# TensorE's loop over pairs of experts in a mixture-of-experts kernel, written out as a straight program

## The chip, the cores and the metric

The kernel runs on one core of one Trainium2 chip. Times are device microseconds of that core, and lower is better. The kernel before takes 859.89 us, the median of three runs (859.68 to 860.04 us).

## The reference, cut to what matters

Tokens (4 batches of 1024, 512 wide) pass a linear layer whose weights and bias are chosen by the batch's category. Each row then goes to one of 8 experts by the largest of 8 softmax probabilities. An expert takes at most 512 tokens, the first that chose it; a token beyond that gets nothing. The result is scaled by the probability and added to the input.

```python
h = einsum('bsd,bdh->bsh', x, W[cat]) + b[cat][:, None, :]
xf = h.reshape(4096, 512)
probs = softmax(xf @ Wr); eidx = argmax(probs); p_tok = probs[eidx]
rank = position of the token among those that chose the same expert
keep = rank < 512                       # capacity 4096 / 8
xe = xf[dispatch]                       # (8, 512, 512)
hid = maximum(einsum('ecd,edf->ecf', xe, W1), 0.0)   # F = 2048
ye = einsum('ecf,efd->ecd', hid, W2) * p
out = x + scatter_add(ye)
```

## The kernel before, in words

Every engine has a program of its own, written out by hand, and the engines meet at semaphores; no scheduler moves anything. All large products are made of float32 values split in two parts, a high part and the rest, and each product is three matmuls (high by high, high by low, low by high: `PARTS`).

The first stage, up to the 153rd microsecond, is a straight program on all engines: the linear layer for 32 tiles of 128 tokens, the routing, and the table of which token goes to which slot. The `pe.wait_ge` calls there compare with constants.

The second stage is the experts, two (`par` 0 and 1) in each of the four iterations of a loop (`pair`), L913. For one expert TensorE makes 16 hidden tiles of 128 x 512 (`j`, L931 to L945): 4 blocks of the contraction times 3 parts is 12 matmuls a tile, into two PSUM banks in turn (`acc_ps`). Between them `second(q)` (L915 to L929) makes 48 matmuls that add a quarter of the hidden rows into the output banks `y_ps`. The order is tiles 0 to 7, second(0), tiles 8 to 11, second(1), tiles 12 to 15, second(2), second(3): 192 matmuls at L941 and 192 at L924 for each expert, so 768 in one iteration.

TensorE waits in this loop for: the split weights (`s_w1lo`, L935, and `s_w2lo`, L916), a freed hidden bank (`s_accf`, L936, which asks that the tile before the last has been taken out), the split inputs of the expert (`s_xelo`, L939), and at the expert's first `second` the outputs of the last expert read (`s_y`, L918). Since `pair` is a register there, each of these thresholds is computed by TensorE's sequencer: register instructions stand among the matmuls.

The other engines go as before in loops of their own: ScalarE takes out a hidden tile (L511) and makes high parts of weights (L459, L465); VectorE makes the low part of the hidden tile and frees its bank (L717), the low parts of weights (L624, L630), and at an expert's end scales the four output tiles and adds the residual (L740). Both loop over pairs, four iterations. SyncE loads the weights in a loop over experts. GpSimd gathers and scatters rows, in a straight program.

Of the kernel before, what the change touches and what calls it, by code (L numbers as in the profile page):

```python
# [17 lines left out]
def moe_kernel(nc, x, x_t, cat, cond_w, cond_wt, cond_b, cond_br, w_r, w_1, w_2, out, h_rows):  # L18
# [8 lines left out]
    E = w_r.shape[1]  # L27
# [41 lines left out]
    with ctx:  # L69
# [674 lines left out]
        def _(pe):  # L744
# [165 lines left out]
                if s < SB - 1:  # L910
                    keep_warm(KEEP_BLOCK)

            with pe.Fori(0, E // 2) as pair:  # L913
                for par in range(2):
                    def second(q):  # L915
                        pe.wait_ge(s_w2lo, pair * (4 * QN) + 2 * (par * QN + q + 1))  # L916
                        if q == 0:
                            pe.wait_ge(s_y, pair * (2 * SB) + par * SB + 1)  # L918
                        pe.wait_ge(s_accf, NT + pair * (2 * FT) + par * FT + QF * (q + 1))
                        for s in range(SB):  # L920
                            for jj in range(QF):
                                j = q * QF + jj
                                for a, w in PARTS:
                                    last = nc.tensor.matmul(y_ps[:, s, :], hts[:, j % HB, a, s * P:(s + 1) * P],  # L924
                                                            w2s[:, q % 2, w, jj, :],
                                                            start=(j == 0 and (a, w) == (HI, HI)),
                                                            stop=(j == FT - 1 and (a, w) == (LO, HI)))
                            if q == QN - 1:
                                last.then_inc(s_f2, 1)  # L929

                    for j in range(FT):  # L931
                        slot, jj = (j // QF) % 2, j % QF
                        tile = pair * (2 * FT) + par * FT + j
                        if jj == 0:
                            pe.wait_ge(s_w1lo, pair * (4 * QN) + 2 * (par * QN + j // QF + 1))  # L935
                        pe.wait_ge(s_accf, NT - 1 + tile)  # L936
                        for k in range(DK):
                            if j == 0:
                                pe.wait_ge(s_xelo, pair * (2 * DK) + par * DK + k + 1)  # L939
                            for w, a in PARTS:  # L940
                                last = nc.tensor.matmul(acc_ps[:, j % 2, :], w1s[slot][:, w, k, jj * P:(jj + 1) * P],  # L941
                                                        xts[:, par, a, k, :],
                                                        start=(k == 0 and (w, a) == (HI, HI)),
                                                        stop=(k == DK - 1 and (w, a) == (LO, HI)))
                        last.then_inc(s_acc, 1)  # L945
                        if jj == QF - 1 and j // QF >= 1:
                            second(j // QF - 1)
                    second(QN - 1)
# [34 lines left out]
```

## Time and profile before

| | before |
|---|---|
| median of three runs | 859.89 us |
| the profiled execution, its own time | 859.88 us |
| its span, first to last instruction | 858.1 us |
| mean granted TensorE clock | 0.993 of 2.4 GHz |
| TensorE matmul busy | 832.0 us (97%) |
| VectorE, ScalarE, GpSimd busy | 47%, 30%, 27% |

The profile is of one execution. Matmuls overlap in the records: one of 512 columns is shown as 389 ns long, while a block of 48 takes 10.88 us from the end of the block before to its own end, so one goes in each 0.227 us. "issue" as a releaser means that the engine stood idle and the profile shows nothing that it waited for. The code that an engine's sequencer runs comes by DMA too, in queues of the kind "instruction".

### The profile page before, as it was taken

How to read it: one execution, taken by the hardware profiler on the slowest of the kernel's cores; microseconds unless marked ns; L12 is line 12 of the kernel's file. 1: busy time of each engine (PE TensorE's matmuls, PEld its weight loads, DVE VectorE, ACT ScalarE, POOL GpSimd, SP SyncE). 2: the span in 40 equal slices, each digit the busy share in tenths (PEclk: the TensorE clock that was granted, in tenths of full speed). 3: DMA queues.
4: the chain of work that ended last, by engine and by line, in shares of the span. 5: the costliest groups of instructions: out<-in, count | busy, mean ns of one | idle time of the engine just before them, and what ended most of it. 6: DMA issues, size and time to landing. Idle time of an engine off the chain costs nothing.

```text
span 858.1 us, 10370 instructions
## 1 busy us (share of the span) xinstructions
PE 832.0 (97%) x3909; PEld 673.2 (78%) x3909; DVE 403.5 (47%) x557; ACT 255.3 (30%) x345; POOL 229.7 (27%) x238
## 2 busy tenths in 40 slices
PE   8959998999999999999999999999999999999997
PEld 5636786788888887888888878888888788888886
DVE  5645663644354434453455336533653275327431
ACT  4412210533143313332233224322432143205320
POOL 2000002724530453036302630173017301021201
PEclk9979999999999999999999999999999999999999
DMA  9847344373435333733263335432544253234201
GB/s 321 293 158 269 137 149 146 138 256 125 133 119 212 123 123 100 245 116 129 91 244 115 132 98 198 151 130 88 196 152 133 95 172 143 86 122 160 102 1 50
DMA packets 60820, 127.68 MB, mean 149 GB/s; under 512 B 8235, under 2 KB 8235, under 8 KB 60258
## 3 DMA queue, kind: packets, MB, share of 16 engines
q1 hardware_dynamic: 46706, 93.35, 30.2%
q0 software_dynamic: 13488, 32.54, 11.8%
q10 hardware_dynamic: 576, 1.05, 0.4%
q8 instruction: 40, 0.66, 0.3%
q14 instruction: 10, 0.08, 0.0%
HBM read 110.13 MB, written 25.17 MB: 158 GB/s over the span
## 4 chain that ended last, share of the span: by engine, by line
PE 94%; DMA 3%; DVE 1%; issue 1%; POOL 0%; ACT 0%; SPq 0%; POOLq 0%
PE acc_ps L941 41%; PE y_ps L924 41%; PE acc_ps L856 6%; PE tp_ps L856 3%; DMA stage<-cond_w 2%; PE tp_ps L783 1%; PE y_ps L792 1%; PE acc_ps L840 1%; DVE select L617 0%; PE tp_ps L758 0%; DMA rows<-h_rows,tok_all 0%; PE y_ps L816 0%; POOL rows L367 0%; PE tp_ps L840 0%; PE y_ps L840 0%
## 5 line engine op out<-in xcount | busy, mean ns | idle before, releaser
L941 PE MATMUL acc_ps<-xt_split,w_split 128*128 128x512 f32 x1536 | 352.9, 389 | 4.6 <-issue 3.5
L924 PE MATMUL y_ps<-w_split,xt_split 128*128 128x512 f32 x1536 | 352.1, 389 | 0.0
L941 PEld LDWEIGHTS acc_ps<-xt_split,w_split 128*128 128x128 f32 x1536 | 288.1, 188 | 65.4 <-issue 4.4
L924 PEld LDWEIGHTS y_ps<-w_split,xt_split 128*128 128x128 f32 x1536 | 288.3, 188 | 59.9
L511 ACT ACTIVATE xt_split<-acc_ps 128x512 fp32r<-128x512 f32 x128 | 76.5, 598 | 420.4 <-PE acc_ps L941 420.4
L717 DVE SCALAR_TENSOR_TENSOR xt_split<-acc_ps,xt_split 128x512 fp32r<-128x512 f32 x128 | 88.6, 692 | 210.8 <-ACT xt_split L511 210.8
L374 POOL DMA_INDIRECT rows<-h_rows,idx_all x112 | 117.1, 1045 | 254.5 <-DVE tp_ps L707 218.2
L624 DVE TENSOR_TENSOR w_split<-stage,w_split 128x1024 fp32r<-128x1024 f32 x66 | 80.9, 1226 | 16.4 <-ACT w_split L459 16.4
L740 DVE SCALAR_TENSOR_TENSOR rows<-y_ps,p_cur,rows 128x512 f32<-128x512 f32 x32 | 24.0, 751 | 133.0 <-PE y_ps L924 133.0
L630 DVE TENSOR_TENSOR w_split<-stage,w_split 128x1024 fp32r<-128x1024 f32 x64 | 78.5, 1226 | 16.4 <-ACT w_split L465 16.4
L406 POOL DMA_INDIRECT out<-rows,put_all x32 | 31.5, 983 | 154.3 <-DVE rows L740 154.3
L459 ACT ACTIVATE w_split<-stage 128x1024 fp32r<-128x1024 f32 x66 | 69.4, 1053 | 0.0
L465 ACT ACTIVATE w_split<-stage 128x1024 fp32r<-128x1024 f32 x64 | 67.4, 1053 | 0.0
L856 PE MATMUL acc_ps<-w_split,xt_split 128*128 128x512 f32 x228 | 57.3, 402 | 0.0
L856 PEld LDWEIGHTS acc_ps<-w_split,xt_split 128*128 128x128 f32 x228 | 42.4, 191 | 13.5 <-issue 3.3
L399 POOL DMA_INDIRECT out<-b_rows,drop_all x32 | 32.8, 1026 | 56.9 <-DMA b_rows<-x 47.8
L367 POOL DMA_INDIRECT rows<-x,tok_all x32 | 34.7, 1085 | 26.3 <-DMA out<-rows,put_all 15.8
L362 POOL DMA_DIRECT2D h_rows<-rows x7 | 5.5, 790 | 119.6 <-DVE rows L566 119.6
L707 DVE STREAM_TRANSPOSE tp_ps<-rows 128x512 f32<-128x512 f32 x32 | 32.8, 1070 | 0.0
L498 ACT ACTIVATE xt_split<-tp_ps 128x512 fp32r<-128x512 f32 x32 | 19.1, 597 | 42.6 <-DVE tp_ps L707 42.6
L566 DVE TENSOR_TENSOR rows<-acc_ps,b_rows 128x512 f32<-128x512 f32 x21 | 14.4, 690 | 26.4 <-PE acc_ps L856 22.7
L856 PE MATMUL tp_ps<-w_split,xt_split 128*128 128x512 f32 x108 | 26.7, 396 | 0.0
(113 smaller groups left out, 260.6 us busy)
## 6 DMA issues: line engine op xcount, KB each, us to landing
stage<-w SPq DMA_DIRECT2D x64, 1024.0 KB, 5.6
b_rows<-x SPq DMA_DIRECT2D x8, 1024.0 KB, 7.7
h_rows<-rows POOLq DMA_DIRECT2D x7, 1024.0 KB, 4.7
stage<-cond_wt SPq DMA_DIRECT2D x4, 1024.0 KB, 7.8
x_more<-x_t SPq DMA_DIRECT2D x4, 1024.0 KB, 7.9
stage<-x_t SPq DMA_DIRECT2D x3, 1024.0 KB, 6.1
stage<-cond_w SPq DMA_DIRECT2D x3, 1024.0 KB, 9.3
rows<-h_rows,idx_all POOLq DMA_INDIRECT x112, 2.7
```

Source lines behind the costliest of these rows:

```text
L367: pool.indirect_dma_start(out=rows[:, which, s, :], out_offset=None, in_=source, in_offset=bass.IndirectOffsetOnAxis(ap=tok_all[:, e, s:s ...
L374: pool.indirect_dma_start(out=h_quart[:, t * P:(t + 1) * P], out_offset=None, in_=h_parts, in_offset=bass.IndirectOffsetOnAxis(ap=idx_all[ ...
L399: pool.indirect_dma_start(out=out, out_offset=bass.IndirectOffsetOnAxis(ap=drop_all[:, BATCH * e + t:BATCH * e + t + 1], axis=0), in_=b_ro ...
L459: nc.scalar.activation(w1s[slot][:, HI, ks, :], stage[:, slot, ks, :], ACTF.Copy).then_inc(s_w1hi, 1)
L465: nc.scalar.activation(w2s[:, slot, HI, ks, :], stage[:, 2 + slot, ks, :], ACTF.Copy).then_inc(s_w2hi, 1)
L511: nc.scalar.activation(hts[:, j % HB, HI, :], acc_ps[:, j % 2, :], ACTF.Relu).then_inc(s_hhi, 1)
L624: nc.vector.tensor_tensor(w1s[slot][:, LO, ks, :], stage[:, slot, ks, :], w1s[slot][:, HI, ks, :].bitcast(f32), ALU.subtract).then_inc(s_w ...
L630: nc.vector.tensor_tensor(w2s[:, slot, LO, ks, :], stage[:, 2 + slot, ks, :], w2s[:, slot, HI, ks, :].bitcast(f32), ALU.subtract).then_inc ...
L717: nc.vector.scalar_tensor_tensor(hts[:, j % HB, LO, :], acc_ps[:, j % 2, :], 0.0, hts[:, j % HB, HI, :].bitcast(f32), ALU.max, ALU.subtrac ...
L856: last = nc.tensor.matmul(cond_bank(n), xts[:, c % 4, a, k, t * P:(t + 1) * P], w2s[:, (c // CPB) % 2, w, k, :], start=(k == 0 and (a, w) ...
L924: last = nc.tensor.matmul(y_ps[:, s, :], hts[:, j % HB, a, s * P:(s + 1) * P], w2s[:, q % 2, w, jj, :], start=(j == 0 and (a, w) == (HI, HI)),
L941: last = nc.tensor.matmul(acc_ps[:, j % 2, :], w1s[slot][:, w, k, jj * P:(jj + 1) * P], xts[:, par, a, k, :], start=(k == 0 and (w, a) == ...
```

## The change

One line. The loop over `pair` on TensorE is no longer a loop of the machine but one of Python, so the builder writes the body four times, one after the other, with `pair` a number.

```diff
-            with pe.Fori(0, E // 2) as pair:
+            for pair in range(E // 2):
                 for par in range(2):
                     def second(q):
                         pe.wait_ge(s_w2lo, pair * (4 * QN) + 2 * (par * QN + q + 1))
```

The 3072 matmuls of the expert stage are the same and in the same order. The branches go, with all register instructions, and waits compare with constants. The instructions of the other four engines stay as they are.

On TensorE, this is the end of the loop's body before, and behind it the body's start, to which the branch goes back (`y_ps` are the output banks, `acc_ps` the hidden ones):

```order
L924 MATMUL y_ps<-w_split,xt_split 128x512 [waits acc_free]
L924 MATMUL y_ps<-w_split,xt_split 128x512 x47
L913 REGISTER_ALU
L913 COMPARE_AND_BRANCH
```

```order
L913 ISA
L936 ISA [waits w1_lo_done]
L939 ISA [waits acc_free]
L941 MATMUL acc_ps<-xt_split,w_split 128x512 [waits xe_lo_done]
L941 MATMUL acc_ps<-xt_split,w_split 128x512 x2
L939 REGISTER_ALU
L941 MATMUL acc_ps<-xt_split,w_split 128x512 [waits xe_lo_done]
```

The first ends in the branch; the second begins with three fused register instructions. At the same place of the changed program, where the second pair of experts begins:

```order
L924 MATMUL y_ps<-w_split,xt_split 128x512 [waits acc_free,w2_lo_done]
L924 MATMUL y_ps<-w_split,xt_split 128x512 x47
L941 MATMUL acc_ps<-xt_split,w_split 128x512 [waits xe_lo_done,acc_free,w1_lo_done]
L941 MATMUL acc_ps<-xt_split,w_split 128x512 x2
L941 MATMUL acc_ps<-xt_split,w_split 128x512 [waits xe_lo_done]
```

The matmuls follow each other with no branch and no register instruction; the same semaphores are waited for. A second place is hidden tile 4 of each expert, on TensorE, where the weights change from one slot to the other. Before:

```order
L935 REGISTER_ALU
L936 REGISTER_ALU [waits w1_lo_done]
L941 MATMUL acc_ps<-xt_split,w_split 128x512 [waits acc_free]
L941 MATMUL acc_ps<-xt_split,w_split 128x512 x11
```

And now:

```order
L941 MATMUL acc_ps<-xt_split,w_split 128x512 [waits acc_free,w1_lo_done]
L941 MATMUL acc_ps<-xt_split,w_split 128x512 x11
```

Before, a register instruction carried the wait for the weights and the matmul the one for the hidden bank (`acc_free`). Now a wait instruction of its own stands ahead of the matmul with `acc_free`, and the matmul carries the wait for the weights. In the first stage nothing moved.

## Rows read from the trace of the kernel before

**Rows 1.** Page, busy time of each engine, share of the span, instructions
```profile
PE 832.0 (97%) x3909; PEld 673.2 (78%) x3909; DVE 403.5 (47%) x557; ACT 255.3 (30%) x345; POOL 229.7 (27%) x238
```
**Rows 2.** Page, costliest groups: busy us, mean ns, idle before, releaser
```profile
L941 PE MATMUL acc_ps<-xt_split,w_split 128*128 128x512 f32 x1536 | 352.9, 389 | 4.6 <-issue 3.5
L924 PE MATMUL y_ps<-w_split,xt_split 128*128 128x512 f32 x1536 | 352.1, 389 | 0.0
```
**Rows 3.** Chain that ended last, whole span: start us, us, what
```profile
152.59 22.09 PE acc_ps L941 x96
174.67 10.88 PE y_ps L924 x48
...
305.23 21.76 PE y_ps L924 x96
326.99 1.73 PE acc_ps L941 x7
328.73 1.31 issue
330.04 20.36 PE acc_ps L941 x89
...
504.31 1.15 issue
...
679.74 1.07 issue
```
**Rows 4.** TensorE's timeline around the three steps back, and between two experts
```profile
239.79 6.51 PE L941 MATMUL acc_ps<-xt_split,w_split 128*128 128x512 f32 x28
...
326.83 1.90 PE L941 MATMUL acc_ps<-xt_split,w_split 128*128 128x512 f32 x7
...
502.56 1.75 PE L941 MATMUL acc_ps<-xt_split,w_split 128*128 128x512 f32 x7
...
677.99 1.75 PE L941 MATMUL acc_ps<-xt_split,w_split 128*128 128x512 f32 x7
```
**Rows 5.** VectorE's timeline: between two experts, three steps back, and the end
```profile
243.34 0.69 DVE L717 SCALAR_TENSOR_TENSOR xt_split<-acc_ps,xt_split 128x512 fp32r<-128x512 f32 x1 [2.60 <-ACT xt_split L511]
...
327.03 0.75 DVE L740 SCALAR_TENSOR_TENSOR rows<-y_ps,p_cur,rows 128x512 f32<-128x512 f32 x1 [1.97 <-PE y_ps L924]
332.03 0.69 DVE L717 SCALAR_TENSOR_TENSOR xt_split<-acc_ps,xt_split 128x512 fp32r<-128x512 f32 x1 [4.25 <-ACT xt_split L511]
...
507.45 0.69 DVE L717 SCALAR_TENSOR_TENSOR xt_split<-acc_ps,xt_split 128x512 fp32r<-128x512 f32 x1 [3.94 <-ACT xt_split L511]
...
682.79 0.69 DVE L717 SCALAR_TENSOR_TENSOR xt_split<-acc_ps,xt_split 128x512 fp32r<-128x512 f32 x1 [3.85 <-ACT xt_split L511]
...
853.52 0.75 DVE L740 SCALAR_TENSOR_TENSOR rows<-y_ps,p_cur,rows 128x512 f32<-128x512 f32 x1 [1.97 <-PE y_ps L924]
```
**Rows 6.** DMA queues, whole run: packets, MB, share of 16 engines
```profile
q8 instruction: 40, 0.66, 0.3%
```
**Rows 7.** The same queue from 332 to 498 us
```profile
q8 instruction: 6, 0.10, 0.2%
```
**Rows 8.** The same queue from 499 to 501 us
```profile
q8 instruction: 1, 0.02, 2.9%
```
**Rows 9.** The same queue from 502 to 504 us
```profile
q8 instruction: 1, 0.02, 4.4%
```
**Rows 10.** The same queue from 506 to 508 us
```profile
q8 instruction: 1, 0.02, 3.0%
```
**Rows 11.** TensorE's waits from 152 to 855 us: total us, times, longest
```profile
PE acc_ps L941 <- issue: 3.5, 3, 1.3
PE acc_ps L941 <- DVE xt_split L693: 1.1, 1, 1.1
```
**Rows 12.** The instruction queue from 0 to 152 us, the first stage
```profile
q8 instruction: 6, 0.10, 0.3%
```
**Rows 13.** Chain from 150 to 175 us: the hand-over into the expert stage
```profile
151.84 0.70 DVE xt_split L693
152.54 0.04 issue
```

## The prediction, made before the changed kernel ran

> **What bounds the kernel now.** I read the engines' busy shares first. TensorE is busy 97% of the span and the next engine, VectorE, 47% [rows 1]: the time is TensorE's own, and only its idle time or fewer, faster matmuls can change it. Then the costliest groups. The two lines of the expert stage, 1536 matmuls each, are most of it; L924 has no idle time before it at all, and L941 has 4.6 us, of which 3.5 us is "issue", time in which TensorE waited for nothing that the profile shows [rows 2]. TensorE's waits from 152 us on say the same in another way: three issue gaps, and one wait of 1.1 us for VectorE when the stage begins [rows 11]. Nothing else ever holds TensorE there: no weight load, no bank, no gather.
>
> The chain tells where the three gaps are. It is TensorE alone, in blocks of 48 matmuls that take 10.88 us each, or 21.76 us for 96. After 305.23 us come the last 96 of the first pair; the second pair begins at 326.99, runs 7 matmuls, and stands still for 1.31 us. The same happens at 504.31 (1.15 us) and at 679.74 (1.07 us) [rows 3]. The reader should see that they come once per step back of the loop, always after 7 matmuls, and nowhere else.
>
> What is TensorE waiting for? The code itself. The queue of kind "instruction" brings 40 packets in the whole run, 0.66 MB, so 16 KB each [rows 6]. Inside a pair they come evenly: 6 in the 166 us from 332 to 498 [rows 7], one in about 28 us, and the stretches of the same length in the other pairs hold 6 too. At the step back there are three close together: one in 499 to 501, one in 502 to 504, one in 506 to 508 [rows 8 to 10], and TensorE, which stopped at 504.31 until 505.46 [rows 3], lies between the second and the third. I read this as: the sequencer, some microseconds ahead of the array, takes the branch and has the piece of code with the body's start fetched (first packet); that piece ends a few instructions after the body's start; the next must be fetched (second packet), and the 7 matmuls at hand run out before it can be used. In the straight stretches the next piece is there before it is needed, and a new piece costs nothing that can be seen: between 174.67 and 326.99 the blocks are 10.88 or 21.76 us long without exception.
>
> **The change, part by part.** First, the branches. Three steps back go. What each costs in all (the gap and small slips beside it) I take from three whole iterations. The last reading of output tiles by VectorE, released by the last matmul of a pair, starts at 327.03 us for the first pair and at 853.52 us for the fourth [rows 5]: 526.49 us for three pairs. Three times 768 matmuls are 48 blocks of 48, at 10.88 us [rows 3], 522.24 us. The excess is 4.25 us, 1.42 us a step back. The gaps alone sum to 1.31 + 1.15 + 1.07 = 3.53 us; the rest is that a matmul's record reaches 0.16 us beyond the start of the next (0.389 less 0.227) three times, and slips such as the one at the first step, where the 7 matmuls take 1.90 us and at the other two 1.75 us [rows 4]. I take 4.25 us, since the time between the two releases holds all of it; 3.53 is its lower bound.
>
> Does something stay behind? In the first iteration, which has no step back, TensorE starts at 152.59 [rows 3] and the second pair at 326.83 [rows 4], 174.24 us for 174.08 us of blocks: 0.16 us, the waits for the first inputs. That remains. If it were the cost of any pair's beginning, the three others would keep it, and the gain would be 3.77 us. For the others the inputs are there long before, so I don't take it.
>
> The fetching of code stays, spread evenly: the stage from 152.59 to 853.5 is then 697 us long, at one packet in 28 us some 25 packets, and with the 6 of the first stage [rows 12] some 31 in place of 40. Each is hidden by the piece that is running. If one were not hidden, it would cost something like the 1.42 us that it costs after a branch.
>
> Second, the register instructions. They stand ahead of the matmuls at each tile, and L924 and L941 show no gap at them [rows 2, 11]: the array has work queued while the sequencer computes. I count them at nothing gained. The wait instructions that take their place at some tiles are counted at nothing too. L924 has such waits already in the loop and no idle time [rows 2]. The one that differs is hidden tile 4: the sequencer now stands at `acc_free`. Between two experts VectorE frees tile 0's bank at 243.34 + 0.69 = 244.03 [rows 5]; tile 2, which needs it, starts two tiles of 2.72 us after 239.79 [rows 4], at 245.23. So 1.20 us of cover at each tile, and a hand-over from VectorE to an idle TensorE took 0.04 us [rows 13]. It would cost only if that hand-over took more than 1.20 us; I bound it by 0 and by 8 tiles times 0.04.
>
> Third, the other engines. ScalarE and VectorE keep their own steps back, and these now lose the cover that TensorE's gap gave them. What must be ready: tile 0 of the new pair must be taken out before tile 2 starts, 5.44 us after the pair's first matmul. In the trace VectorE ended it at 332.72, 508.14 and 683.48 [rows 5], which is 5.89, 5.58 and 5.49 us after 326.83, 502.56 and 677.99 [rows 4]. So even if VectorE could not have been a moment earlier, TensorE would wait only 0.45 + 0.14 + 0.05 us, and three hand-overs, 0.76 us in all. But VectorE was held there by ScalarE, and ScalarE by TensorE itself: VectorE had been idle for 4.25 us [rows 5], and without the gap would have been called 1.3 us earlier. I take 0 and keep 0.76 for the range. Weight loads, gathers and scatters are set off by work that runs behind TensorE, so they move with it; none of them made TensorE wait once [rows 11], and per pair of 175 us they get 1.4 us less.
>
> The end is unchanged: from VectorE's last reading at 853.52 to the end of the span, 4.6 us.
>
> Sum: 859.88 us (the profiled execution; the median of the runs is 859.89, the same) less 4.25 is 855.63 us. Bounds: with 4.5 us gained, 855.4; with 3.53 us gained and all 0.76 + 0.32 us of new waits, 857.4.
>
> The page "Runtime: NRT & Kernel Launch" of the Trainium skill, in "Instruction fetch mechanics", says that a taken branch whose target is not in the window at hand makes the sequencer fetch it first, and that prefetch is purely sequential; by this rule the gaps go with the branches, and the trace agrees with three packets round each one. The same section gives TensorE an instruction memory of 128 KiB, 2048 instructions. The loop's body has fewer (1536 for its 768 matmuls and weight loads, and some tens of others), so if it stayed in that memory a step back would fetch nothing; the trace disagrees, since the 6 packets come in every pair. By the first rule the sum stands at 855.6 us; by the second the gap would not be a fetch, and rival (a) would hold.
>
> **The rivals.** (a) The gap is not the code's fetch but some other cost of beginning a pair, and stays: the change then doesn't do what it says. What speaks for it: "issue" names no cause. Against: the beginning of the first pair lacks it, 174.24 us against 175.73 for the second (502.56 less 326.83), and so does the middle of a pair, where the same waits stand. Only what the branch itself takes would go. In the trace that could be the slip of 0.15 us (1.90 less 1.75) at the first step [rows 4]; three of them make 0.45 us, and the time 859.4 us. A reading of the page "Advanced Engine Details and Errata", "Control Flow Timing", leads the same way: it has a compare-and-branch at about 108 ns, by which three would give back about 0.3 us; no row here shows such a duration by itself. Chance 6%.
>
> (b) The straight program can't be fetched in time: slower. Place: each of the about 25 new pieces of code of the stage. Price: if each stops TensorE as the one after a branch does, 25 x 1.42 = 35.5 us, less 4.25, and the time is 891 us. It decides from 0.17 us a piece on. For it: the fetch after a branch takes longer than 7 matmuls. Against: TensorE ran through 24 such pieces inside the four iterations and 6 in the straight first stage [rows 12], and no gap recurs with them. Chance 3%.
>
> (c) A wait takes the gap's place: VectorE's or ScalarE's own step back, uncovered. At most 0.76 us by the working above, so the time is 856.4 us, still faster. Chance 9%.
>
> **How the numbers follow.** The forecast, 855.6 us, has 82%, with (c) 9%, (a) 6% and (b) 3%. From the run spread of 0.2 us either way, a little more for the same first stage in another build, and the bounds above, the range is 855.0 to 857.0. A difference of less than 0.2%, 1.7 us, can't be told from no change here; the forecast and (c) lie beyond it, (a) within, (b) on the other side. So faster 0.91, same 0.06, slower 0.03.
>
> **What would show it right or wrong.** In the changed profile: no issue gap at L941 at all, or none over 0.2 us; the pairs 174.1 us apart; the span 853.9 us; about 31 packets in the instruction queue, evenly spaced; VectorE's idle time before the first L717 of a pair back near 2.6 us. Wrong: a gap of about 1 us after a few matmuls of a pair, or a wait for L717 at the third tile of a pair (c), or short gaps every 28 us (b).

## The result, and the profile after

The changed kernel takes 857.01 us (median of 8 executions, 854.65 to 858.47), the kernel before beside it 859.96 us (8 executions). The ratio is 0.9962, 95% interval 0.9947 to 0.9977: faster, by 2.95 us between the medians. Forecast were 855.6 us and a range of 855.0 to 857.0; the median lies a hundredth beyond its upper end. By the ratio the gain is 3.3 us, where 4.25 were forecast. Two later comparisons on other chips gave 0.9948 (0.9934 to 0.9963) and 0.9947 (0.9931 to 0.9964), which is 4.5 us; between the medians it is 4.0 and 4.8 us. All ratios and intervals leave out three executions of a slower state (893.68 us with 16 added instructions, 4214.43 us with 224, 2163.0 us of the kernel before); the medians given do not.

The costliest groups of the changed kernel's page, busy us, mean ns, idle before and its releaser. They answer to [rows 2]:

```profile
L941 PE MATMUL acc_ps<-xt_split,w_split 128*128 128x512 f32 x1536 | 352.2, 389 | 1.1 <-DVE xt_split L693 1.1
L924 PE MATMUL y_ps<-w_split,xt_split 128*128 128x512 f32 x1536 | 352.1, 389 | 0.0
```

The matmuls cost what they did. The 3.5 us of "issue" before L941 is gone, and what is left is the wait for the first inputs of the stage, which was there before [rows 11]. The chain (start, us, what) answers to [rows 3]:

```profile
154.34 22.05 PE acc_ps L941 x96
...
328.71 21.76 PE acc_ps L941 x96
...
502.79 21.76 PE acc_ps L941 x96
...
676.87 21.76 PE acc_ps L941 x96
```

The reader is to see blocks of 96 at a pair's beginning, whole, where there were 7 matmuls, a gap and 89. Pairs follow each other at 174.08 us (502.79 less 328.71, 676.87 less 502.79). VectorE's timeline shows the first hidden tile of the second pair and the last reading of outputs, as in [rows 5]:

```profile
332.10 0.69 DVE L717 SCALAR_TENSOR_TENSOR xt_split<-acc_ps,xt_split 128x512 fp32r<-128x512 f32 x1 [2.60 <-ACT xt_split L511]
...
850.98 0.75 DVE L740 SCALAR_TENSOR_TENSOR rows<-y_ps,p_cur,rows 128x512 f32<-128x512 f32 x1 [1.97 <-PE y_ps L924]
```

VectorE's idle time there fell from 4.25 to 2.60 us, what it is in the middle of a pair. And the instruction queue over the whole run, which answers to [rows 6]:

```profile
q8 instruction: 31, 0.51, 0.2%
```

From the first matmul of the expert stage to VectorE's last reading it was 853.52 less 152.59, 700.93 us; now it is 850.98 less 154.34, 696.64 us. So the stage gave back 4.29 us where 4.25 were forecast. But it starts 1.75 us later (154.34, not 152.59), and so the span fell only from 858.1 to 855.6 us. The loss lies in a first stage whose instructions are the same. Below, "the expert stage" is always this interval.

### The profile page after: what moved, and what is told of

Its sections match the earlier page's. It is cut to its first block, busy times and chain, and to the rows that moved or that the text cites. A ratio compares the mean times of both kernels' runs of the same rounds, so it can differ in the third digit from the quotient of the medians.

```text
span 855.6 us, 10205 instructions
## 1 busy us (share of the span) xinstructions
PE 832.2 (97%) x3909; PEld 674.9 (79%) x3909; DVE 403.5 (47%) x557; ACT 255.2 (30%) x345; POOL 229.7 (27%) x238
## 3 DMA queue, kind: packets, MB, share of 16 engines
q10 hardware_dynamic: 576, 1.05, 0.4%
## 4 chain that ended last, share of the span: by engine, by line
PE 95%; DMA 3%; DVE 1%; issue 0%; ACT 0%; SPq 0%; POOL 0%; POOLq 0%
PE acc_ps L941 41%; PE y_ps L924 41%; PE acc_ps L856 6%; PE tp_ps L856 3%; DMA stage<-cond_w 2%; PE tp_ps L783 1%; PE y_ps L792 1%; PE acc_ps L840 1%; DVE select L617 0%; PE tp_ps L758 0%; DMA rows<-h_rows,tok_all 0%; PE y_ps L816 0%; PE y_ps L888 0%; PE acc_ps L865 0%; PE tp_ps L840 0%
## 5 line engine op out<-in xcount | busy, mean ns | idle before, releaser
L941 PE MATMUL acc_ps<-xt_split,w_split 128*128 128x512 f32 x1536 | 352.2, 389 | 1.1 <-DVE xt_split L693 1.1
L941 PEld LDWEIGHTS acc_ps<-xt_split,w_split 128*128 128x128 f32 x1536 | 288.3, 188 | 61.1 <-issue 1.3
L717 DVE SCALAR_TENSOR_TENSOR xt_split<-acc_ps,xt_split 128x512 fp32r<-128x512 f32 x128 | 88.5, 692 | 206.9 <-ACT xt_split L511 206.9
```

The lines of the kernel that those rows point to most:

```text
L717: nc.vector.scalar_tensor_tensor(hts[:, j % HB, LO, :], acc_ps[:, j % 2, :], 0.0, hts[:, j % HB, HI, :].bitcast(f32), ALU.max, ALU.subtrac ...
```

## The experiments

The text on record speaks of "pieces of code": what one packet of the instruction queue brings. The straight program has 7,919 TensorE instructions in its trace and takes 31 packets of 16 KB, about 256 instructions each. The loop's body has 1,593 (768 matmuls with a weight load each, and 57 others), which is 6.2 pieces. Of these, 19 stand ahead of the point where TensorE stops in the kernel before: three register instructions, seven matmuls with their weight loads, and two more register instructions. So the first piece ends some 20 instructions behind the body's start, and the body lies in 1 + 7 = 8 pieces. The places given below all follow from this 20. Three things could make the gap: the step back itself, the fetch of the branch's target, or the fetch of the piece behind it. They differ in what happens if the loop is kept and the code is only shifted. All kernels here compute the reference in full.

**The kernel before, unchanged.**

> The kernel before, unchanged, to see how its own time spreads. Theory (the step back costs 1.42 us, and the first stage varies by itself from one execution to the next): the time from the first matmul of the expert stage to the last is 701 us again, three gaps of 1.1 to 1.3 us after 7 matmuls, median 859.9 us; whatever differs between executions lies before the expert stage (loads of the first weights, the clock in the two long waits). Rival (the loop's version has a steadier first stage than the straight one): all executions within 0.3 us of 859.9.

Measured: 867.25 us beside 866.64 for the same kernel, ratio 1.0014 (0.9999 to 1.0029). This chip is slower than the first, so neither the 859.9 us nor the 701 us of the theory was met. On it both versions of the kernel also wait some 0.7 us at L941 six times, which the profiles on the other chips don't show; the profile puts five of the six here, and two in the changed kernel, to the freeing of a bank (L717), and the others to nothing that it shows. The gaps are there, 1.60, 1.20 and 1.28 us after 7 matmuls, and 40 packets; the expert stage takes 707.70 us. The executions run from 865.85 to 872.73 us, so the rival of a steadier loop version is out.

**24 instructions that do nothing, ahead of the loop.**

```diff
+            for _ in range(48):
+                pe.wait_ge(s_mask, 13)
             with pe.Fori(0, E // 2) as pair:
```

Two such waits make one instruction. They were satisfied long before.

> The kernel before, loop kept, with 24 more instructions that do nothing (waits already satisfied) on TensorE just ahead of the loop, so that the body's start stands 24 places later in the code. Theory (the gap is the fetch of the SECOND 16 KB piece of code after the branch, which comes too late since the first ends some 20 instructions behind the body's start): the body now starts at the head of a piece, the piece after it is needed only 28 us later, and the three gaps go although every branch stays: expert stage 696.6 us plus at most three slips of 0.25 us, median about 856, as the straight program. Rival A (the gap is the cost of the branch or of the pair's beginning): three gaps of 1.1 to 1.3 us stay, 859.9 us. Rival B (it is the fetch of the branch's target): the gaps stay or move to the very first matmul, 859.9 us.

Measured: 864.96 us, ratio 0.9983 (0.9962 to 1.0004); expert stage 702.61 us, 5.1 us shorter than in the kernel before on this chip. No gap at any step back, with every branch in place. By time alone this run can't be told from no change, since the interval reaches 1.0004. But the instruction queue says something that the theory hadn't:

```profile
q8 instruction: 13, 0.21, 0.1%
```

Thirteen packets for the whole run, and none after 321 us: from the second pair on the body is not fetched again at all. Shifted by 24, it starts 4 instructions behind the head of a piece and lies in 7 pieces; before, it lay in 8. So this run can't tell a late second piece from code that stayed. The wait before the first L941 was 2.37 us, in place of 1.05, so the 24 instructions cost some 1.3 us where they stood. That is part of why the total gained less than the stage.

**16 such instructions.** The same edit with 32 waits.

> As with 24, but 16 such instructions, so that the piece ends 4 instructions behind the body's start. Theory: TensorE has no matmul at hand in place of 7 while the second piece comes, so each step back costs 7 x 0.227 = 1.59 us more, 3.0 in place of 1.42: the gap stands at the first matmul of the pair, expert stage 705.6 us, median 859.9 + 4.8 = 864.7 us. Rival A and B: 859.9 us.

Measured: 882.01 us (878.03 to 893.68), ratio 1.0184 (1.0140 to 1.0227), some 16 us by the ratio and 12 us between the profiled executions (878.16 and 865.92 us), where the theory gave 4.8. TensorE's timeline where the second, third and fourth pair begin:

```profile
335.97 24.68 PE L944 MATMUL acc_ps<-xt_split,w_split 128*128 128x512 f32 x96 [3.27 <-issue]
...
517.48 21.95 PE L944 MATMUL acc_ps<-xt_split,w_split 128*128 128x512 f32 x96 [2.48 <-issue]
...
695.95 23.55 PE L944 MATMUL acc_ps<-xt_split,w_split 128*128 128x512 f32 x96 [2.23 <-issue]
```

The gap stands at the first matmul and is longer, as the theory has it, with 40 packets. What it had missed is behind the gap: the 96 matmuls take up to 24.68 us in place of 21.95. The windows around 336 us (stretch, TensorE busy, matmuls, granted clock, DMA share, GB/s) tell why:

```profile
336.00:339.00 3.00, 3.00 (x8) 0.50 0.19 69
339.00:342.00 3.00, 3.00 (x9) 0.53 0.60 158
342.00:345.00 3.00, 3.00 (x15) 1.00 0.66 191
```

After 3.27 us of idle time TensorE's clock stood at its lower level, 1.2 GHz, for some 6 us: a longer gap can cost the clock too. It is not by length alone: behind the gap of 2.48 us the granted clock stayed at 1.00, behind the one of 2.23 us it was 0.63 and 0.80 in the next two stretches of 3 us. The expert stage took 717.82 us, 10.1 more than on the same chip before: 8.0 us of gaps against 4.1, some 4.3 us of slow clock behind two of them, and 1.5 us of two waits in the first pair. In this profile the stage also starts 2.1 us later. That late start isn't explained, nor is why others of its executions took as long as 889.43 us.

**The changed kernel again.**

> The changed kernel, unchanged again, on the same chip as the kernel before. Theory: the expert stage takes 696.6 us again without any gap, and the scatter of the earlier runs (854.7 to 858.5) lies in the first stage, the same scatter that the kernel before has: median of enough runs 855.7 us, ratio 0.995. Rival (the straight program makes the first stage about 1.3 us longer, where a step of clock or a load falls otherwise): the first matmul of the expert stage starts about 1 to 2 us later than in the kernel before in this profile too, and the ratio stays at 0.9965.

Measured: 862.62 us, ratio 0.9948 (0.9934 to 0.9963). Expert stage 702.30 us, against 707.70: 5.40 us less, of which 4.08 are the three gaps of that profile. This profile starts it at 155.36 us, 3.5 us later than the kernel before, so a late start came a second time, while the ratio was already the forecast one.

**224 such instructions, spread over two idle times of the first stage.** This is the run that separates the late second piece from code that stays.

```diff
             keep_warm(KEEP_FIRST)
+            for _ in range(200):
+                pe.wait_ge(s_mask, 2)
...
             def route(c):
+                if c == CPB:
+                    for _ in range(248):
+                        pe.wait_ge(s_mask, 13)
```

> The loop kept, and 224 instructions that do nothing on TensorE, spread over its two idle times in the first stage (before the first tiles and before the ninth-microsecond wait at the second batch), so that the loop's body starts 52 places ahead of the end of a 16 KB piece of code (256 instructions) in place of 20, and still lies in 8 pieces, as in the kernel before. Theory 1 (the fetch of the second piece comes too late, and a body in 8 pieces doesn't stay in the memory): 40 or 41 packets again, all fetched anew at each step back, but some 20 matmuls (4.5 us) at hand while the second comes: no gap, expert stage as in the straight program. Theory 2 (what took the gaps away with 24 was only that a body in 7 pieces isn't fetched again): the gaps stay wherever the body is fetched again, 1.4 us each. If only 13 or 14 packets come, the limit isn't 8 pieces.

Measured: 41 packets, so the body was fetched anew for each pair. The instruction queue, and TensorE's waits from 160.5 to 862 us:

```profile
q8 instruction: 41, 0.67, 0.3%
PE acc_ps L946 <- DVE xt_split L693: 1.0, 1, 1.0
```

No gap. The expert stage took 696.99 us, that of the straight program within 0.4. The time, 864.43 us (ratio 1.0036, 1.0023 to 1.0050), is the price of 224 instructions in the first stage: the expert stage starts at 161.18 us. They were not free in the idle times, as I had thought they would be. Theory 1 stands: the gap is the second piece coming too late, and a step back with a fetch costs nothing if some 20 matmuls stand before the piece's end.

The start times of the packets in the traces give the margin. In all thirteen gaps (three each in the two profiles of the kernel before and in those with 8 and with 16 instructions, one in the loop with one step back) TensorE goes on 2.3 to 3.0 us after the second piece's packet has started (at the second step back of the kernel before, packet 502.61, matmul 505.46). Here that packet starts at 335.53 us, as the pair's first matmul does, so by the same times the piece can be used at 338.6 at the latest, while the matmuls at hand last until about 340.5 (an estimate: 22 of them at 0.227 us).

**One step back in place of three.**

```diff
-            with pe.Fori(0, E // 2) as pair:
-                for par in range(2):
+            with pe.Fori(0, E // 4) as quad:
+                for half in range(2):
+                    pair = quad * 2 + half
+                    for par in range(2):
```

> The loop with two iterations of two pairs each, so one step back in place of three; the body starts at the same place of the code. Theory: one gap of 1.1 to 1.6 us after 7 matmuls of the third pair, none at the second and fourth; the expert stage 2.8 us shorter than in the kernel before; some 34 packets. Rival (a pair's beginning costs the gap): three gaps.

Measured: 858.41 us, ratio 0.9974 (0.9961 to 0.9986), 34 packets, and one gap, at the third pair. Its waits from 300 us on:

```profile
PE acc_ps L943 <- issue: 1.4, 1, 1.4
```

Expert stage 698.25 us: 2.7 less than before, 1.65 more than straight. One step back costs one gap; the rival, a gap at each pair's beginning, is out.

**The 24 instructions at a place where TensorE is idle** (behind the first `keep_warm`, where the last run had 100 of its 224).

> The loop kept, and the 24 instructions that do nothing put into TensorE's idle time before the first tiles, where they hold nothing up. Theory: 13 packets and no gap at a step back, as with the 24 just ahead of the loop, and the 1.3 us that those 24 cost there at the stage's beginning are gone too: as fast as the straight program, ratio 0.995 to 0.9965. Rival (the 24 do something at their place, such as giving the other engines time): three gaps, 1.000.

Measured: 856.22 us, ratio 0.9950 (0.9932 to 0.9969), and 13 packets. TensorE's waits from 152.5 to 855 us:

```profile
PE acc_ps L943 <- DVE xt_split L693: 1.1, 1, 1.1
```

Expert stage 696.69 us, no gap. A loop with its branches and all its register instructions is as fast as the straight program (696.60 to 696.64 us), when its body lies so that it needs no new code: branches and registers together cost under 0.1 us.

**8 such instructions, ahead of the loop.**

> The loop kept, with 8 instructions that do nothing just ahead of it, so that the first piece of code ends 12 instructions behind the body's start (20 in the kernel before, 4 with 16 added). Theory: 4 matmuls are at hand in place of 7, so each gap comes after 4 matmuls and is 3 x 0.227 = 0.7 us longer, 1.8 to 2.0 us where it was 1.1 to 1.3; 40 packets; the kernel 2 us slower, and more where the longer idle time also drops the clock, as it did after the gap of 3.27 us. Rival (length of the gap doesn't depend on the place): gaps of 1.1 to 1.3 us.

Measured: 866.18 us, ratio 1.0064 (1.0041 to 1.0088), 40 packets; that is 5.7 us slower where the theory gave 2 and more if the clock dropped. The chain in the profile of this kernel, its pieces at the three steps back:

```profile
329.78 1.00 PE acc_ps L944 x4
330.78 2.20 issue
...
508.09 1.09 PE acc_ps L944 x4
509.17 2.19 issue
...
686.34 0.91 PE acc_ps L944 x4
687.25 1.73 issue
```

Four matmuls, and gaps of 2.04 us in the mean where 7 matmuls left 1.18 [rows 3]. Three matmuls fewer at 0.227 us are 0.68, the difference is 0.86. The stage took 707.07 us, 10.5 more than straight. Of this 6.1 us are gaps; most of the rest is the clock, since the 92 matmuls behind the first two gaps took 22.79 and 22.66 us, and 21.15 behind the third. The granted clock was 0.87 and 0.79 in the two stretches of 5 us from 330 us on, around the first gap.

**The changed kernel a third time.**

> The changed kernel once more, beside the kernel before on the same chip. Theory (4.3 us go in the expert stage, and the first stage took some 1.0 to 1.3 us more in the two earlier comparisons): expert stage 696.6 us from the first to the last matmul and no gap; ratio 0.9955 to 0.997. If the first stage's loss was chance, the ratio is 0.995 and the profile's expert stage starts before 153 us.

Measured: 855.62 us (855.06 to 855.83) beside 860.46, ratio 0.9947 (0.9931 to 0.9964). That this is the forecast time to the hundredth is luck: on this chip the kernel before took 0.6 us more than the time from which the forecast was worked out. The expert stage starts at 152.38 us and takes 696.60 us. So the late start of the first profile is not in every execution of the changed kernel.

**Two versions beyond the change**, both straight, against the slow clock after TensorE's wait of 9 us in the first stage.

```diff
             def route(c):
+                if c == CPB:
+                    pe.wait_ge(s_ltc, c)
+                    for _ in range(36):
+                        nc.tensor.matmul(turn_ps, ones[:, :], zeros[:, :], start=True, stop=True)
```

> The changed, straight program, with 36 matmuls that multiply by zeros and whose result is overwritten put into TensorE's 9 us wait at the second batch (into the routing bank, before the routing product of tile 10). Theory (part of the scatter of the first stage is TensorE's clock, which goes to half after that wait: 12 matmuls at L856 took 4.6 us in the profile after, 3.9 before, and 2.9 where the clock is full): the 8 routing matmuls and the 12 behind take 1 and 2.9 us, and the first stage is 1.5 to 2.6 us shorter; the ratio 0.9925 to 0.994. Rival (the wait, not the clock, sets it): no change against the straight program, 0.9955.

Measured: 855.65 us, ratio 0.9942 (0.9921 to 0.9962). The timeline shows the routing products and the tile behind them, at a granted clock of 1.00:

```profile
55.69 1.06 PE L787 MATMUL tp_ps<-x_more,m 128*32 128x512 f32 x8 [0.62 <-DVE bias_g L556]
56.69 3.02 PE L860 MATMUL acc_ps<-w_split,xt_split 128*128 128x512 f32 x12
```

These two groups took 1.93 and 4.00 us in the kernel before, at 0.65. So the clock came back as the theory has it, but the forecast ratio was just missed, and the first stage was not 1.5 us shorter: the expert stage starts at 152.25 us, and at 151.29 in the loop with one step back on the same chip. The second version also raises `KEEP_GATHER` from 20 to 27:

> The straight program with the 36 zero matmuls in the wait at the second batch, and 27 in place of 20 before the first gathered rows, which fill most of TensorE's 2 us of idle time there. Theory: in the profile with 36 alone the clock still fell to half after that idle time (4 transposes and 2 zero matmuls took 1.10 and 1.06 us, where they take 0.72 and 0.59 at full clock); with it filled they take the short times, the expert stage starts 0 to 0.7 us earlier; ratio 0.9925 to 0.994. Rival (the rows' arrival sets the end of this chain, so the clock there costs nothing): as with the 36 alone, 0.994.

Measured: 855.38 us, ratio 0.9949 (0.9929 to 0.9968). The groups of four transposes took their short times, 0.72 to 0.75 us, but the expert stage started at 152.56 us, no earlier. Neither version can be told from the plain straight program at 0.9947: the intervals overlap. What the clock gives back in the routing is 1.85 us there (5.93 less 4.08), and where it is lost again before the expert stage wasn't followed up.

## Why the prediction was right, and where it wasn't

**The branches: 4.25 us.** Right in size and place. The stage gave 4.29 us in the first profile, and 4.33 in the third (700.93 less 696.60). The loop with one step back kept 1.65 us of it, a little more than a third. The lower bound of 3.53 us from the gaps alone was too low, as the working had it.

**The cause.** The prediction read three packets of code around each step back as target, second piece, third piece, and the gap as the second coming too late. The shifts show it: the gap begins after 7 matmuls with the body as it was, after 4 with 8 instructions more, at the first matmul with 16, and is gone with 52 instructions before the piece's end although the code is fetched anew (the run with 224).

**The rule of the 2048 instructions.** Here the prediction was wrong. It said that the trace disagrees with the Trainium skill's page "Runtime: NRT & Kernel Launch", section "Instruction fetch mechanics", since the body of fewer instructions was fetched in every pair. What counts is not only the number of instructions but in how many pieces they lie. With the body in 7 pieces it stayed: 13 packets in place of 40. With the body in 8, nine packets come in each pair, so one piece more than the body has. The ninth is the piece behind the body: in the kernel before it starts 5.8 us ahead of the next target's packet, and with 224 instructions, where only some 5 instructions of the body lie in the eighth piece and not some 37, it starts 2.1 us ahead. The page's memory of 128 KiB, 8 pieces of 16 KiB, fits both: 7 and 1 go in, 8 and 1 don't. That the memory's size is the reason is my reading; the runs show the 7, the 8 and the packets. This changed neither the sum nor the rival it was tied to, but it hid the cheapest remedy.

**The fetch of the straight program, registers and waits: nothing.** Right: no idle time of TensorE in the stage but the first, 31 packets as forecast, and tile 4's wait costs nothing. The loop that keeps its branches and registers and has no gap takes 696.69 us, which bounds the registers' part at 0.1 us.

**The other engines' own steps back: 0 taken, 0.76 bound.** Right at 0. VectorE was called after 2.60 us and was ready.

**The first stage: taken as unchanged.** This is the term that was off in the first comparison. It was 1.75 us longer in that profile: the first weights' transfer took 5.29 us in the chain and not 4.65; the second batch's took 11.09 and not 10.71; and the 12 matmuls behind the long wait took 4.62 and not 3.93, at the lower clock. In the third profile the stage ended 0.21 us earlier than in the first profile of the kernel before. The same program thus started the experts at 154.34, 155.36 and 152.38 us, and the kernel before at 152.59 and 151.91. I take it for scatter between executions, which the loads and the clock make, and this is argued and not shown: two of the three samples of the straight program were late, and why it was so on those chips stays open. For it speaks that the two later comparisons gave 4.5 us by the ratio, at least what the stage gave in the first profile. The range allowed for 1.4 us of it, and for a median of 8 that was a little short; the working's own upper bound, 857.4 us, would have held the median, and the range was drawn in to 857.0 without a row for it. So the mechanism and the stage's 4.25 us were right, and the time of the first comparison was off by 1.4 us that no term of the sum held.

**Rivals.** (a), the gap stays: out, no gap. (b), the straight code isn't fetched in time: out, 31 packets without a gap. (c), a new wait of up to 0.76 us: out, none.

## What to carry to other kernels

Idle time that a profile calls "issue", a few instructions behind the point to which a loop steps back, is worth comparing with the packets of the instruction queue: here they pointed to the cause, which shifting the code then showed, and counting them also shows whether the body is fetched again. A loop can be freed of the gap by writing it out, but also by moving where its body lies. Shifting code by a few instructions moved this kernel between 0.995 and 1.018 of its time, so a difference between two versions of a loop can come from where their bodies lie and not from what was changed in them.

## What the runs showed that I had not expected

- A body of 1,593 instructions was fetched once when it lay in 7 pieces (13 packets in the run) and four times when it lay in 8 (40 and 41 packets).
- A gap of 3.27 us in steady work put TensorE at 0.50 of its clock for some 6 us; after the gap of 1.31 us in the kernel before it stayed at full clock. Between these lengths it went either way: 1.00 behind 2.48 us, but 0.63 behind 2.23 us, both with 16 instructions added.
- Waits that are already satisfied are not free in number: 24 of the two-fold wait instructions added about 1.3 us (2.37 less 1.05) where TensorE was about to begin. It is no fixed price for each: at the same place 16 added 0.3 us and 8 added nothing.
